# q and k of two tiles as one 2x2 block product in Strassen's form: seven products in place of eight, with another order of steps

## What is computed

```python
q = (x @ Wq.T + bq).reshape(B, S, H, D)      # H = 16, D = 32
k = (x @ Wk.T + bk).reshape(B, S, H, D)
v = (x @ Wv.T + bv).reshape(B, S, H, D)
q = _apply_rope(q, cos, sin)
k = _apply_rope(k, cos, sin)
qk = jnp.einsum('bshd,bstd->bsht', q, k) / jnp.sqrt(jnp.float32(D))
out = jnp.einsum('bsht,bstd->bshd', jax.nn.softmax(qk, axis=-1), v)
x = _layernorm(x + swap(out) @ Wo.T + bo)    # swap: heads and rows exchanged
hdn = jax.nn.silu(x @ gate_w.T * gate_s) * (x @ up_w.T * up_s)
x = _layernorm(x + hdn @ down_w.T * down_s)
```

## Time and profile before

| what | value |
|---|---|
| median of 3 runs | 1719.14 us (1717.97 to 1721.07) |
| the profiled execution | 1720.26 us |
| its span | 1718.5 us |
| mean granted clock of PE | 0.997 of full speed |
| PE busy | 1692.1 us, 98% |
| DVE, ACT, POOL busy | 73%, 54%, 24% |
| first matmul at | 8.02 us |
| first feed-forward product at | 812.2 us |

### The profile page before, as it was taken

How to read it: one execution, slowest core, us unless ns; L and a number is a source line. 1 busy time by engine, 2 the same in 40 slices (tenths; PEclk the granted TensorE clock), 3 DMA queues, 4 the chain that set the end, 5 groups by cost and what they waited for, 6 DMA issues and landing times.

```text
span 1718.5 us, 39846 instructions
## 1 busy us (share of the span) xinstructions
PE 1692.1 (98%) x15138; PEld 1391.2 (81%) x15138; DVE 1251.0 (73%) x1844; ACT 935.1 (54%) x1458; POOL 412.2 (24%) x444
## 2 busy tenths in 40 slices
PE   8999999999999999999999999999999999999997
PEld 6778888888888888887788888888888888888886
DVE  5778778777877877787857677676676766767656
ACT  5555555555455555546545554554555545556453
POOL 2433433343343334334100201102011020110112
PEclk9999999999999999999999999999999999999999
DMA  6488868777887887787762644435535345354351
GB/s 204 99 189 180 178 159 166 177 171 158 178 182 182 188 194 174 158 174 183 212 219 75 206 156 137 156 101 192 159 119 173 118 150 169 99 193 141 105 178 62
DMA packets 438707, 275.52 MB, mean 160 GB/s; under 512 B 257280, under 2 KB 377216, under 8 KB 438656
## 3 DMA queue, kind: packets, MB, share of 16 engines
q1 hardware_dynamic: 438512, 274.61, 60.5%
q10 hardware_dynamic: 144, 0.26, 0.0%
HBM read 181.74 MB, written 93.06 MB: 160 GB/s over the span
## 4 chain that ended last, share of the span: by engine, by line
PE 96%; DVE 2%; issue 1%; DMA 0%; ACT 0%; POOL 0%; POOLq 0%; SPq 0%; DVEq 0%; ACTq 0%
PE ps_x L632 14%; PE ps_x L633 13%; PE ps_x L636 13%; PE ps_s L802 9%; PE ps_s L807 9%; PE ps_x L802 7%; PE ps_x L807 7%; PE ps_x L813 5%; PE ps_x L817 4%; PE ps_s L709 3%; PE ps_a L666 3%; PE ps_a L817 2%; PE ps_a L813 2%; PE ps_s L813 2%; PE ps_s L817 2%
## 5 line engine op out<-in xcount | busy, mean ns | idle before, releaser
L632 PE MATMUL ps_x<-wqkv_hi,xc_hi 128*128 128x512 f32 x768 | 303.6, 395 | 8.1 <-POOL xc_lo L1203 8.0
L633 PE MATMUL ps_x<-wqkv_lo,xc_hi 128*128 128x512 f32 x768 | 299.8, 390 | 0.0
L636 PE MATMUL ps_x<-wqkv_hi,xc_lo 128*128 128x512 f32 x768 | 299.7, 390 | 0.0
L802 PE MATMUL ps_s<-x_hi,slot 128*128 128x512 f32 x672 | 264.1, 393 | 0.7 <-DVE hid L1576 0.3
L807 PE MATMUL ps_s<-x_lo,slot 128*128 128x512 f32 x672 | 261.8, 390 | 0.0
L956 ACT ACTIVATE kX<-kT 32x512 f32<-32x512 f32 x256 | 160.6, 627 | 111.4 <-DVE kT L1395 103.4
L802 PE MATMUL ps_x<-x_hi,slot 128*128 128x512 f32 x560 | 218.9, 391 | 1.5 <-ACT sg L1068 0.8
L807 PE MATMUL ps_x<-x_lo,slot 128*128 128x512 f32 x560 | 218.0, 389 | 0.0
L1327 POOL TENSOR_TENSOR z<-z,xr 128x512 f32<-128x512 f32 x60 | 77.3, 1315 | 480.5 <-DVE z L1645 480.5
L632 PEld LDWEIGHTS ps_x<-wqkv_hi,xc_hi 128*128 128x128 f32 x768 | 144.7, 188 | 40.0 <-ACT xc_hi L939 8.0
L636 PEld LDWEIGHTS ps_x<-wqkv_hi,xc_lo 128*128 128x128 f32 x768 | 144.8, 188 | 30.7
(11 more groups left out here) (117 smaller groups left out, 3354.5 us busy)
## 6 DMA issues: line engine op xcount, KB each, us to landing
slot<-gu_hi SPq DMA_DIRECT2D x88, 896.0 KB, 5.1
xc<-x_cols SPq DMA_DIRECT2D x32, 512.0 KB, 4.6
v_rows<-v_in SPq DMA_DIRECT2D x32, 512.0 KB, 3.1
...
res<-x_rows SPq DMA_DIRECT2D x64, 256.0 KB, 2.7
...
x_cols<-x_turn SPq DMA_DIRECT2D x128, 128.0 KB, 2.5
wide<-x_cols SPq DMA_DIRECT2D x64, 256.0 KB, 5.1
```

The costliest lines, as they stand in the source:

```text
L632: pe.matmul(out, hi[:, k], w_hi[w][:, k], start=(k == 0), stop=False)
L633: pe.matmul(out, hi[:, k], w_lo[w][:, k], start=False, stop=False)
L636: last = pe.matmul(out, lo[:, k], w_hi[w][:, k], start=False, stop=(k == KE - 1))
L802: pe.matmul(out[:, :], slot[:, WEIGHTS[i], cols], x_hi[:, i, k], start=start, stop=False, skip_group_check=True)
```

## The change

Two tiles of x, each with its 512 columns in two halves, are a 2x2 block matrix A; the weights of k and q, each in two halves of rows, are a 2x2 block matrix B. Their product holds k and q of both tiles. The changed kernel makes it from seven block products Q1 to Q7 with sums of blocks of A and of B (Winograd's form of Strassen's method): A11 B11, A12 B21, and five products in which sums stand. One block product contracts over 256 and is 6 matmuls of 128x512. PSUM takes the additions of the form in part: Q1, Q6, Q7 and Q4 are added up in one bank (BANK_X), and DVE reads the bank in between; Q2 has its own (BANK_Z), Q5 and Q3 share a third (BANK_W). The value and head projections stay as they were.

New work: four sums of x blocks for each unit (`sums_of_tiles`, POOL, 128x256), their high parts (`high_of_sum`, ACT) and low parts (`low_of_sum`, POOL); seven operations on DVE that take q and k out of PSUM in place of four (`first_sum_of_qk` and the like). Once, at the start: sums of the weight blocks (`first_block_sum` and the like) and high and low parts of seven blocks of 256 rows in place of eight. The order of the steps is new on all engines: a step of PE is now Q1, Q2, weighing (unit u-2), scores (u-1), value projection of tile 0, Q6, value projection of tile 1, Q7, heads of tile 0 (u-2), Q4, Q5, heads of tile 1, Q3. SP loads the tiles of the feed-forward half in the last step, since their place in SBUF is that of x and its parts; before it loaded them from step 20 on.

The core of the diff:

```diff
+            def block_of_qk(q, m, ahead=None):
+                t = {Q1: 0, Q2: 0, Q4: 1}.get(q)
...
+                if q == Q1:
+                    at_least(pe, k1_made, m)
+                elif q == Q2:
+                    at_least(pe, k0_made, m)
+                    at_least(pe, y_done, 2 * (m - 3) + 1)
+                elif q == Q6:
+                    pe.wait_ge(qk_s1_made, m + 1)
+                elif q == Q7:
+                    pe.wait_ge(qk_u2_made, m + 1)
+                elif q == Q4:
+                    pe.wait_ge(qk_u3_made, m + 1)
+                elif q == Q5:
+                    pe.wait_ge(v_biased, 3 if isinstance(m, int) and m < 2 else 2 * m + 1)
+                    at_least(pe, q0_made, m)
+                else:
+                    pe.wait_ge(q1_made, m + 1)
+                hi, lo = operand(q, m)
+                for k in range(KH):
+                    last = three(ps_x[QK_BANK[q]][:, :], hi[:, k], lo[:, k], wb_hi[:, q, k], wb_lo[:, q, k],
+                                 k == 0 and q in (Q1, Q2, Q5), k == KH - 1, ahead if k == KH - 1 else None)
+                last.then_inc(qk_done[q], 1)
...
+            def step(u):
+                def small_inputs():
+                    inputs_of_av(u - 2)
+                    inputs_of_score(u - 1)
+
+                last = isinstance(u, int) and u == UNITS - 1
+                block_of_qk(Q1, u)
+                block_of_qk(Q2, u, small_inputs)
+                weigh_values(u - 2)
+                score(u - 1)
+                project_v(u, 0)
+                block_of_qk(Q6, u)
+                project_v(u, 1)
+                block_of_qk(Q7, u)
+                project_heads(u - 2, 0)
+                block_of_qk(Q4, u)
+                block_of_qk(Q5, u)
+                project_heads(u - 2, 1)
+                if last:
+                    inputs_of_av(u - 1)
+                    weigh_values(u - 1)
+                block_of_qk(Q3, u)
...
+            def sums_of_tiles(m):
...
+                a11, a12, a21, a22 = (raw_of(m)[:, i] for i in range(4))
+                s1, s2, s3, s4 = (x_sum[:, i] for i in range(4))
+                pool.tensor_tensor(s1, a21, a22, ALU.add).then_inc(x_summed, 1)
+                pool.tensor_tensor(s3, a11, a21, ALU.subtract).then_inc(x_summed, 1)
+                pool.wait_ge(x_summed, 4 * m + 1)
+                pool.tensor_tensor(s2, s1, a11, ALU.subtract).then_inc(x_summed, 1)
+                pool.wait_ge(x_summed, 4 * m + 3)
+                pool.tensor_tensor(s4, a12, s2, ALU.subtract).then_inc(x_summed, 1)
...
+            def begin_step(u):
+                q_of_first(u - 1)
+                turn_q(u - 1, 0)
+
+            def rest_of_step(u):
+                first_sum_of_qk(u)
+                aggregate(u - 3)
+                k_of_first(u)
+                turn_k(u, 0)
+                low_of_heads(u - 2)
+                subtract_top(u - 1)
+                shift_of(u - 3)
+                add_v_bias(u, 0)
+                second_sum_of_qk(u)
+                sums_of_prob(u - 1)
+                scale_prob(u - 1)
+                add_v_bias(u, 1)
+                third_sum_of_qk(u)
+                turn_prob(u - 1)
+                turn_x1(u - 3)
+                add_residual(u - 2, (0,))
+                k_of_second(u)
+                q_of_second(u)
+                turn_k(u, 1)
+                turn_q(u, 1)
+                add_residual(u - 2, (1,))
...
+            store_v(0)
             load_x(2)
-            ffn_slabs(1)
+            load_slab(0)
+            store_v(1)
             load_v(0)
+            load_slab(1)
             load_residual(0)
-            store_v(1)
             load_x(3)
+            store_slab(0)
             load_v(1)
-            ffn_slabs(2)
-            load_residual(1)
-            ffn_slabs(3)
+            load_slab(2)
             store_v(2)
```

More of the change, by code:

```diff
@@ L391, in load_v @@
             def load_v(m):
+                if m == 0:
+                    sp.wait_ge(b_lo_done2, LOW_BY_POOL.index(Q5) + 1)
                 at_least(sp, av_done, m)
@@ L754, in _ @@
+            project_heads(0, 1)
+            with pe.Fori(OPENING - 1, UNITS - 1) as i:
+                step(i)
+            step(UNITS - 1)
+            project_heads(UNITS - 2, 0)
+            inputs_of_score(UNITS - 1)
+            score(UNITS - 1)
             pe.wait_ge(lo_reduced, 1)
-            pe.wait_ge(biased[2], 2 * UNITS)
-            pe.matmul(ps_x[0][0:1, 0:1], lo_top1[:, :], ones[:, :], start=True, stop=True).then_inc(lo_joined, 1)
-            project_heads(UNITS + 1, UNITS - 2, (1,))
+            pe.wait_ge(k1_made, UNITS)
@@ L1278, in _ @@
+            low_of_tile(2, 0)
+            low_of_tile(2, 1)
+            for k in range(KE):
+                low_of_wo(k)
+            sums_of_tiles(2)
+            for q in S_ORDER:
+                low_of_sum(2, q)
             sums_of_slab(0)
@@ new lines, in step @@
+            def step(u):
+                begin_step(u)
+                rest_of_step(u)
+            for k in range(KE):
+                low_of_wv(k)
+            low_of_block(Q1)
+            low_of_block(Q2)
+            add_v_bias(0, 0)
+            add_v_bias(0, 1)
+            first_sum_of_qk(0)
+            k_of_first(0)
+            first_block_sum()
+            second_block_sum()
+            fourth_block_sum()
+            low_of_block(Q6)
+            low_of_block(Q7)
+            add_v_bias(1, 0)
@@ L1572, in sum_c22 @@
+            add_residual(0, (0, 1))
+            rest_of_step(3)
+            with dve.Fori(OPENING, UNITS) as i:
+                step(i)
+            begin_step(UNITS)
             def sum_c22(n, j):
```

911 lines of the change are left out of this document (495 added, 416 removed).

## The result

The changed kernel takes **1709.59 us** (median of 5 runs, 1706.68 to 1711.18) against 1719.14 us before: a ratio of 0.9942, 95% interval 0.9927 to 0.9956. It is faster by 9.6 us, as forecast in sign and inside the range (1680 to 1712), but the forecast was 1698, a gain of 20.6: less than half of it came. The profiled execution has a span of 1707.9 us.

The account below looks back on a forecast made before the run. PE was taken to bound the loop. Six fewer matmuls a unit could save 43.5 us; with losses in opening and passage 20.6 remained, taking 1719.14 to 1698, range 1680 to 1712.

Parts of the forecast that it names:

- The loop: Steady attention loop: PE stays the bound, a unit falls from 24.98 to 23.62 us, 43.5 us in all; DVE 92% busy.
- The collision of the scaling with POOL: Steady loop: DVE's scaling of probabilities meets POOL's 0.4 us pieces, adding 0.4 us of DVE time a step, within the slack.
- The slower rival: Steady loop: scaling meets POOL's 1.93 us slab operation each step, step 25 us, total 1737; chance 9%.
- The opening: Start of the attention half: Q6 at 24.4, first scores about 37.1, step 4 at 115.4 us after waits and half clock.
- the very rule: DVE instructions with two SBUF inputs and GpSimd instructions reading SBUF block each other fully; applied to the scaling of probabilities.
- The first two of the three chains: After the first scores: POOL and ACT work delays unit 1's scores, 2.3 us idle; slab 1 and residual delay first heads, 7.4.
- The third chain: After the first heads: slab 2's transfer, sums and copies delay Q7 of step 3 to 101.0 from 95.8, about 5 us idle.
- The 5 us of idle in step 3: Sign that the forecast is right: PE idle some 5 us in step 3, as Q7 waits for DVE's second sum.
- The 3.0 us that I added behind Q7: Before the steady loop: 1.6 us for the clock drop after idle and 1.4 us for loss on entering the loop.
- The passage: Attention to feed-forward: PE waits 2.9 us before unit 30's heads; P7 comes 42.0 us into step 31, plus 1.6 for clock.

Follow-up runs that it names:

- The run with the slabs early: Against the changed kernel, the opening's slabs are prepared as early as data allow, loads ahead of residuals and tiles, heads of unit 0 earlier on ACT: 1703.62 us.
- the kernel with the sums apart: Against the changed kernel, DVE makes all weight-block sums and low parts, and POOL's sums for unit 1 wait for six low parts: 1708.55 us.

## Why the prediction was right and wrong

**The loop: right.** Six matmuls fewer were to give 23.62 us a unit; it is 23.57. DVE is busy for 92% and PE never waits. The collision of the scaling with POOL is there, as forecast, and small (groups of DVE and POOL, 400 to 700 us: count, busy us, mean ns):

```profile
L1625 DVE TENSOR_TENSOR prob<-prob,over 128x1024 f32<-128x1024 f32 x12 | 16.7, 1395 | 0.4
```

```profile
L1391 POOL TENSOR_TENSOR f_all<-f_all 128x88 f32<-128x88 f32 x12 | 16.4, 1363 | 0.0
```

The scaling takes 1.40 in place of 1.21: I had added 0.4. POOL pays more: one of its 88-column operations in each slab takes 1.36 in place of 0.38. The slower rival, in which the scaling meets the long slab operation, did not occur in any step.

**The opening: the term that failed.** The step is "DVE makes the block sums from 19.5 to 23.2, so Q6 starts at 24.4". I had priced those operations as if each engine were alone, though the paragraph just ahead of it states the very rule that forbids it: I applied it to the scaling and not to the place where DVE and POOL both work on weight blocks of 128x1024. The sums ended at 26.67, Q6 came at 30.22, 5.8 us late, and half clock over 30 to 39 and PE's waits on DVE made 10.0 us of it by the first scores. Without POOL's reading Q6 is at 25.81 and the scores at 38.25: nearly the forecast. So the mechanism was known and one place of it missed.

The first two of the three chains behind were sized well. From the first scores to the first heads I had 40.6 us, measured 41.3; I had PE idle ahead of the heads for 7.4 us, measured 7.19. Their order was also right, as the chain of waits shows.

**The third chain: one link left out.** From the first heads to Q7 of step 3 I had 23.3 us; it took 26.3. I let ACT's copy of slab 2 follow POOL's sums at once, from 90.8 to 91.7. The changed kernel's timelines of SP, POOL, ACT and DVE there, and PE's:

```profile
99.00 0.85 SPq L437 DMA_DIRECT2D gu_hi<-f_hi  x1
...
100.47 0.39 POOL L1395 TENSOR_TENSOR f_all<-f_all 128x88 f32<-128x88 f32 x1
...
104.41 0.87 ACT L1061 ACTIVATE f_hi<-f_all 128x792 fp32r<-128x792 f32 x1 [7.68 <-issue]
...
113.60 0.68 DVE L1557 TENSOR_TENSOR qk_in<-ps_x,bias 128x512 f32<-128x512 f32 x1
```

```profile
104.40 0.93 PE L748 MATMUL ps_s<-kX,qT 64*32 64x64 f32 x42 [2.85 <-issue]
```

POOL's sums end at 100.86, the copy starts at 104.41, 3.5 us later. It also waits until the high part of slab 1 is stored from the tile that it writes (`f_hi_stored` in `high_of_slab`). SP issues that store behind the eleven pieces of slab 2, its second part at 99.00, and this one landed 5.3 us after its issue: 104.3. I had put that link at nothing. The run with the slabs early has the stores ahead of it, and its copy of slab 2 starts without a wait (75.44); the store was not moved by itself.

Q7 hangs on DVE's second sum, which ends at 114.28, and starts at 114.69. So PE's stop of 2.85 us in the scores of step 3, the half clock over 105 to 110.5 behind it and that over 88 to 94 behind the first heads (24 matmuls in 7.66 us, 5.2 at full clock) lie, all but 0.4 us at most, in time that this chain sets. Of the opening's drops of the clock only the one over 30 to 39 lengthens the way to step 4. The 5 us of idle in step 3 that I named as a sign did not show as a wait at Q7. The 3.0 us that I added behind Q7 for the clock and the entry into the loop were not needed: from Q7 to weighing of step 4 it took 14.3 us against 17.1. From there to weighing of step 20 at 506.14 it is 377.1 us, 16 x 23.57, so nothing is lost there either. That is how 10.0 + 0.7 + 3.0 - 2.8 makes the 10.9 of step 4.

**The passage: right in kind, 1.8 us short.** The wait before the heads of unit 30 was forecast at 2.9 and is 2.75. From weighing of step 31 to P7 I had 42.0 + 1.6 - 2.72 = 40.9 us; it took 42.69. Most of the difference is a stop of PE in the middle of the scores of step 31, for which the profile shows no wait:

```profile
769.68 0.46 PE L748 MATMUL ps_s<-kX,qT 64*32 64x64 f32 x19 [1.61 <-issue]
```

**The sum.** Like points of the two kernels (units 0 to 3 projected): 100.24 before, 129.03 - 2.72 = 126.3 after. The opening loses 26.1 us and not 15.2; P7 comes 817.41 - 808.09 = 9.3 earlier and not 20.6; the whole is 9.6 earlier. Of the miss of 11.3, 10.9 are the opening and 1.8 the passage, and the loop gives 1.4 back.

**Open.** Why PE stops in the middle of the small matmuls (1.5 to 3.6 us, no wait in the profile), in the opening and at the end alone, is not shown. It costs time by itself and in some places clock behind it; the kernel before has it too (3.04 in the weighing and then half clock). And why the changed kernel keeps its full clock after that gap while the kernel with the sums apart does not was not tested by itself.
